# A second attention whose scores stand by keys on partitions, with GpSimd subtracting the maximum

## The reference

```python
x = x + _L0_conv_ref(_gn(x), ...)        # 8 heads, mask, depthwise convolution
t = _to_tokens(x)
t = t + _L1_attn_ref(_ln_t(t), Wq, bq, Wk, bk, Wv, bv)
t = t + _L1_ffn_ref(_ln_t(t), ...)       # two of eight experts for each image

def _L1_attn_ref(x, Wq, bq, Wk, bk, Wv, bv):
    q, k, v = x @ Wq + bq, x @ Wk + bk, x @ Wv + bv
    scores = jnp.einsum('btd,bsd->bts', q, k)
    attn = jax.nn.softmax(scores, axis=-1)
    return jnp.einsum('bts,bsd->btd', attn, v)
```

## Time and profile before

| | us |
|---|---|
| median of three executions | 3510.87 |
| the profiled execution | 3511.96 |
| its span, first to last instruction | 3510.2 |
| TensorE busy | 3403.2 (97%) |
| VectorE busy | 2635.0 (75%) |
| ScalarE busy | 2015.6 (57%) |
| GpSimd busy | 1645.1 (47%) |
| second attention, first scores to last values | 2575.4 to 3347.8 |

### The profile page before, as it was taken

One profiled execution on the slowest core, in us unless ns is written; L12 is line 12 of the kernel. 1 busy time (PEld: TensorE's weight loads), 2 busy tenths in 40 slices (PEclk: granted clock), 3 DMA queues, 4 the chain that ended last, 5 costly groups with the idle time before them and its releaser, 6 DMA issues. The chain is left out here.

```text
span 3510.2 us, 94134 instructions
## 1 busy us (share of the span) xinstructions
PE 3403.2 (97%) x30646; PEld 2643.6 (75%) x30646; DVE 2635.0 (75%) x6494; ACT 2015.6 (57%) x3642; POOL 1645.1 (47%) x863
## 2 busy tenths in 40 slices
PE   8799999999999999999999999999799999999978
PEld 5477777777777777777777777777578888888867
DVE  8688888888888888888888888888666675654457
ACT  4466666666666666666666666666435454455533
POOL 5566656556556556656656655655400001005112
PEclk9899999999999999999999999999899999999989
DMA  7642242234224224222422422222331020100011
GB/s 266 194 133 94 72 135 94 72 106 123 73 99 129 72 92 136 73 92 100 109 92 94 115 92 94 81 91 94 106 99 58 15 85 4 39 1 1 1 44 42
DMA packets 111794, 308.21 MB, mean 88 GB/s; under 512 B 11592, under 2 KB 72955, under 8 KB 91163
## 3 DMA queue, kind: packets, MB, share of 16 engines
q1 hardware_dynamic: 110629, 306.27, 27.9%
q10 hardware_dynamic: 1054, 0.48, 0.1%
HBM read 252.38 MB, written 54.31 MB: 87 GB/s over the span
## 5 line engine op out<-in xcount | busy, mean ns | idle before, releaser
L730 ACT ACTIVATE c_PT<-c_Tps 128x512 f32<-128x512 f32 x2592 | 1428.3, 604 | 877.8 <-PE c_Tps L860 815.7
L795 DVE CUSTOM_DVE_ANT_0 c_S<-c_Sps,mask_tiles 128x768 f32<-128x768 f32 x1728 | 1619.3, 956 | 412.6 <-PE c_Sps L849 371.8
L698 POOL TENSOR_SCALAR c_S<-c_S,c_row_max 128x2304 f32<-128x2304 f32 x576 | 1414.0, 2455 | 950.6 <-DVE c_row_max L806 950.6
L860 PE MATMUL c_Tps<-ident,c_S 128*128 128x128 f32 x10368 | 1400.8, 273 | 4.1 <-ACT c_PT L730 4.1
L860 PEld LDWEIGHTS c_Tps<-ident,c_S 128*128 128x128 f32 x10368 | 1229.7, 140 | 152.1 <-ACT c_PT L730 9.7
L849 PE MATMUL c_Sps<-c_K,c_Q 96*128 (+1 forms) x3456 | 854.6, 328 | 29.0 <-DVE c_part_max L795 14.6
L873 PE MATMUL c_Ops<-c_PT,c_V 128*32 128x256 f32 x10368 | 619.2, 382 | 0.8 <-ACT c_PT L730 0.8
L873 PEld LDWEIGHTS c_Ops<-c_PT,c_V 128*32 128x32 f32 x10368 | 307.4, 109 | 243.6 <-issue 51.1
L849 PEld LDWEIGHTS c_Sps<-c_K,c_Q 96*128 96x128 bf16 x3456 | 315.2, 98 | 188.4 <-issue 144.1
L1463 DVE TENSOR_SCALAR_CACHE_REDUCE l_S<-l_Sps,l_v 128x384 f32<-128x384 f32 x432 | 259.8, 618 | 252.9 <-PE l_Sps L1264 249.3
L1148 ACT ACTIVATE ln2T<-l_Tps 128x384 f32<-128x384 f32 x432 | 196.5, 491 | 363.6 <-PE l_Tps L1287 363.6
(11 more groups left out here) (223 smaller groups left out, 1644.2 us busy)
## 6 DMA issues: line engine op xcount, KB each, us to landing
mask_tiles<-in_mask SPq DMA_DIRECT2D x144, 1152.0 KB, 7.7
numerators<-c_O SPq DMA_DIRECT2D x288, 64.0 KB
mask_tiles<-numerators SPq DMA_DIRECT2D x7, 2304.0 KB, 8.5
q_parts<-c_PT SPq DMA_DIRECT2D x12, 576.0 KB, 4.4
k_parts<-c_PT SPq DMA_DIRECT2D x12, 576.0 KB
c_Q<-q_parts SPq DMA_DIRECT2D x71, 96.0 KB
c_vpad<-v_padded SPq DMA_DIRECT2D x8, 756.0 KB, 14.8
c_K<-k_parts SPq DMA_DIRECT2D x7, 864.0 KB, 8.6
```

The lines of the kernel that those rows point to most:

```text
L698: pool.tensor_scalar(S[:, slot, :], S[:, slot, :], -1.0, row_max[:, slot:slot + 1], ALU.mult, ALU.add).then_inc(shifted, 1)
L730: act.activation(dst, src, ACT.Exp, scale=-1.0).then_inc(exp_done, 1)
L795: dve.tensor_tensor_reduce(out=S[:, r % ROW_SLOTS, cols(CH, c)].rearrange("p (k n) -> p k n", k=2), in0=Sps[:, n % S_SLOTS, :, 0:GW], in1= ...
L860: last = pe.transpose(Tps[:, g % T_SLOTS, cols(P, k)], S[:, (2 * b + t) % ROW_SLOTS, cols(P, kt)], ident[:, :])
```

## The change

For a query tile, the scores now come out with keys on partitions: 18 matmuls of 128 keys (stationary, from lnT) by 128 queries (moving, read straight from qT; no staging copy), in the orientation in which the values need them. The 18 transposes of the exponentials go. ScalarE copies the raw scores from PSUM to one of three slots of SBUF (the two rows of S and the former PT). The maximum of a query now lies across keys on partitions and across 18 tiles, so:

- VectorE takes the maximum over nine key tiles, twice (half_maximum, a tensor_reduce whose inner step is 128 floats), and joins the two (key_maximum, 128 x 128).
- TensorE turns that (turn_max); VectorE reduces it to one number a query and spreads it over 128 columns (query_maximum); TensorE turns it back (spread_max); ScalarE copies it to SBUF (take_shift).
- GpSimd subtracts it from the 18 x 128 scores in two tensor_tensor of 1152 columns (subtract_max), and ScalarE makes the exponentials in two halves.

A column of ones behind the values gives the sum (129 columns instead of 128). The scores run two tiles ahead instead of one (AHEAD = 2), and PSUM has four banks for them (T_SLOTS = 4) and two for the turned maxima. GpSimd's bias groups are spread over the tiles 0 to 5, and normal over the tiles of the last image, at most two groups a tile. In the loop of VectorE the preparation still stands behind the tiles of the same numbers, now after key_maximum.

```diff
-            def scores(b, qt, t, groups=range(NG)):
...
-                    pe.matmul(Sps[:, g % S_SLOTS, 0:GW], q_tile[:, t, :], lnT[:, bass.ds((b % 2) * N + g * GW, GW)],
...
+                        last = pe.matmul(Tps[:, (n + g) % T_SLOTS, cols(P, k)], lnT[:, bass.ds((b % 2) * N + (g * GB + k) * P, P)], query_tile,
+                                         start=True, stop=True)
...
-                        block_t = pe.transpose(Tps[:, g % T_SLOTS, cols(P, k)], S[:, t, cols(P, g * GB + k)], ident[:, :])
...
+                if j + AHEAD < ALL:
+                    scores(j + AHEAD, range(4))
+                    spread_max(j + 1)
+                    scores(j + AHEAD, range(4, NG))
+                values(j, 0)
+                if j + AHEAD == ALL:
+                    spread_max(j + 1)
+                values(j, 1)
+                if j + AHEAD < ALL:
+                    turn_max(j + AHEAD)
...
+            def subtract_max(j):
+                pool.wait_ge(shift_in, j + 1)
+                for half in HALVES:
+                    part = keys_by[j % P_SLOTS][:, half.start:half.stop, :]
+                    pool.tensor_tensor(part, part, shift[:, :, :].to_broadcast([P, len(half), P]), ALU.subtract).then_inc(shifted, 1)
...
+                if j + AHEAD < ALL:
+                    take_scores(j + AHEAD, range(4))
+                if j + 1 < ALL:
+                    take_shift(j + 1)
+                if j + AHEAD < ALL:
+                    take_scores(j + AHEAD, range(4, NG))
+                if j + 1 < ALL:
+                    for half in range(2):
+                        exponentials(j + 1, half)
+                if b + 1 < B and qt == TRANSPOSE - 1:
+                    deviations(b + 1)
...
+            def half_maximum(j, half):
+                dve.wait_ge(t_taken, scores_at(j) + NG * (half + 1) // 2 + T_SLOTS)
+                part = keys_by[j % P_SLOTS][:, HALVES[half].start:HALVES[half].stop, :].rearrange("p t q -> p q t")
+                dve.tensor_reduce(half_max[:, half, :], part, AX.X, ALU.max).then_inc(half_step, 1)
...
+            def key_maximum(j):
+                dve.wait_ge(half_step, 2 * (j + 1))
+                dve.tensor_tensor(key_max[:, j % 2, :], half_max[:, 0, :], half_max[:, 1, :], ALU.max).then_inc(key_max_ready, 1)
...
+            for j in range(ALL):
+                b, qt = j // TILES, j % TILES
+                if j:
+                    take_row(j - 1)
...
+                if j and j + 1 < ALL:
+                    query_maximum(j + 1)
+                if j:
+                    row_statistics(j - 1)
+                if j + AHEAD < ALL:
+                    half_maximum(j + AHEAD, 0)
+                    half_maximum(j + AHEAD, 1)
+                    key_maximum(j + AHEAD)
+                if b + 1 < B:
+                    if qt == 0:
+                        invert(b + 1)
...
```

More of the change, by code:

```diff
@@ L1324, in _ @@
[L1324 to L1330 removed]
+            scores(0, range(NG))
+            scores(1, range(3))
```

436 lines of the change are left out of this document (208 added, 228 removed).

## The result

| | before | after |
|---|---|---|
| median (lowest to highest), us | 3510.06 (3508.09 to 3511.88) | 3518.18 (3516.83 to 3520.58) |
| ratio, with its 95% interval | | 1.0024 (1.0014 to 1.0035) |
| span of the profiled execution, us | 3510.2 | 3516.5 |
| scores to scores in a plain tile, us | 9.86 | 9.22 |
| first scores of the stage to the end of the last value, us | 772.4 | 783.1 |

The forecast was 3519. The stage is 10.7 us longer, and it began 4.0 us earlier, at 2571.45 instead of 2575.41; the rest of the program is as it was. So the 4.0 us lie within that scatter, and I count them as no part of the change.

What follows compares the result with a forecast made beforehand. TensorE was taken to bound the second attention. Plain tiles and ends -64, side work +61, GpSimd in the last image +12 gave +9 on 3511.96 us; 3519 was forecast, range 3455 to 3565, the forecast's own 3500 to 3538.

Steps and rivals of the forecast that it cites:

- 69 plain tiles: Second attention, tiles without side work: each falls from 9.86 to 8.95 us, 63 us less in all.
- the ends: Filling and draining of the tile pipe: 30 us against 31.5 before, counted as 1 us less.
- side work of three images: VectorE's preparation of the next image delays spread_max and TensorE: 19.7 us an image, 2 in the filling pipe, 61 us.
- GpSimd in the last image: normal, 4.7 us for two groups, makes ten tiles 10.4 us long against 8.95: 12 us more.
- TensorE's part: A tile falls from 90 to 74 passes, 8.3 us at 0.112 each; 112 us would go if all else were hidden.
- The rival that no passes are saved: TensorE's 128-column matmuls with fresh weights are slower than wide ones, so the passes do not go; chance 0.04.
- GpSimd's half: One subtract_max tensor_tensor of 1152 columns: 2.5 us, ends 2.3 and 3.0, so 5.0 us a tile.
- The strided rival: half_maximum's 128-float step is slow: at twice 1.34 us plain tiles stay, stalled ones grow some 16 us, 3535; chance 0.06.
- Key_maximum first: Rival: key_maximum gets its turn at the boundary of GpSimd's halves; tile 8.45 us, time 3485, range 3465 to 3500; chance 0.24.
- the forecast's state: key_maximum asks just after GpSimd began its second half and stands until it ends; tile 8.95 us; chance 0.33.
- the stall before the transposes of ln: normalise waits behind the square root, itself behind tile 11's exponentials: TensorE stands 5.8 us in each of three images.
- the slower rival: TensorE's clock halves at stalls, 5 us each, 15 or twice that: 3535 to 3550; chance 0.17 together with dear GpSimd halves.

Runs made afterwards that it cites:

- the last kernel: No key_maximum, side work ahead of half_maximum, bias six tiles earlier, last-image normal() moved from GpSimd to VectorE, against the kernel before: 3438.47 us, ratio 0.9797.

## Why the prediction held, and where it was lucky

The sum was -64 + 61 + 12 = +9, and the stage gave +10.7. Its terms, from the spacings of tiles:

| term | predicted, us | measured, us |
|---|---|---|
| 69 plain tiles | 69 x (8.95 - 9.86) = -63 | 69 x (9.22 - 9.86) = -44 |
| the ends | -1 | 33.9 - 31.4 = +2.5 |
| side work of three images | 59 + 2 = +61 | 98.3 - 52.8 = +45.5 |
| GpSimd in the last image | +12 | 14.8 - 8.0 = +7 |
| sum | +9 | +11 |

The measured terms of the last two rows are what the tiles are longer than plain ones, after less before. They hold TensorE's passes for the preparation and the expert transposes, which both kernels have. The ends after are 21.35 us to the start of tile 1 (2571.45 to 2592.80), where 19 were predicted, and 12.5 for the last two tiles, where 11 were.

The total is right by luck in the sizes: 19 us too much gain from the tiles stood against 16 us too much loss from the side work and 5 in the last image, and the ends are 3.5 us worse. The mechanisms were the ones named.

**TensorE's part.** A pass is 0.112 us for 128-column matmuls with fresh weights too: the 24 score passes of the plain tile start at 3332.81 and the next matmul at 3335.49, 2.68 / 24 = 0.112. 75 passes fill a tile of 8.37 and 74 one of 8.26, in the kernels where TensorE is the bound. The rival that no passes are saved falls.

**GpSimd's half, the mis-sized term.** 2.5 us were taken between 2.3 and 3.0, by proportion from 768 columns; 2.64 were measured. A tile is two halves and 3.95 by the prediction's own layout. In the plain tile above GpSimd starts 3.62 us behind the first scores (3332.81), works 5.25, and the next scores start 0.36 after it, at 3342.04: 5.25 + 3.98 = 9.23. So the 3.95 was right, and 0.27 x 69 = 19 us is the error of the tiles, nearly all of it in the halves. The row of 768 columns reads one bf16 input beside an f32; whether that makes it cheaper, no run tells.

The estimate of 2.6 from the Trainium skill (GPSIMD Engine Reference, Performance versus the Vector engine) was nearer, and its sum, 14 us longer, would have had this term nearly right. In plain proportion the page's 4497 ns for 2048 columns make 2.53 at 1152, an estimate that is no better than the row's.

**Who waits for whom.** Shown by the kernel without key_maximum: 55 us of waits go with one instruction. The Trainium skill (SBUF — State Buffer, Who interferes with whom) exempts tensor_reduce from the lock, which no row of before showed; the trace after agrees, with 2.12 to 2.23 us for all 144 half_maximum, most of them beside a running GpSimd half. The bias locks as predicted: the first product of finish_half starts 0.1 us behind a bias and takes 2.16 us instead of 1.34 (at 2823.94). What the prediction leaves out are operations with one input and output both in SBUF, which stand too: the copy and the tensor_scalar of the last kernel.

**half_maximum, wrong and without effect.** 1.34 us were taken from sum_half, 2.20 measured. The strided rival had it at two times with plain tiles unchanged, and that holds: with reading in order alone the time is 2.2 us less, and the intervals of the two ratios overlap, because it is not enough to reach the boundary. The 16 us put on stalled tiles for it do not show.

**Key_maximum first.** The margin was not the 0.1 us of the prediction but 0.85, since half_maximum is slow. So this kernel was further from the rival than the prediction thought; but, as the kernel that reads in order shows, without the stride it is still in the forecast's state, at the very boundary. In plain tiles the mechanism is as described: asked 0.4 us ahead of the boundary VectorE gets the turn, asked at the boundary it stands 2.75 us. The tile that follows is 8.26, where 8.45 was worked out: the loop through ScalarE and GpSimd does not bind. The 3485 of the rival is 3476 in the kernel that is in that state (which leaves part of the reduction out).

**Side work, the order right, the size too large.** The waits behind it, without TensorE's passes, are 16.3 us an image where 19.7 were predicted, and 3.1 in the filling pipe where 2 were, 52 in all. From these comes off what the prediction put at nothing: the kernel before had 1.5 us of waits an image in the same tiles, and its passes for the preparation took some 0.7 us more, together 6.5 us in three images. Per image, now: invert 0.63 us (1.4 predicted), the sums 2.6 and 2.75 (3.4 each), the finishes 1.5 and 0.7 (2.3, 1.3), statistics 1.5 (2.1), the stall before the transposes of ln 6.55 (5.8). The short ones are each 0.6 to 0.8 less. Half of this can be read off. spread_max stands 2.84 us behind turn_max in the plain tile (2.7 predicted) and take_row with query_maximum takes 1.17 (3332.52 to 3333.69; 1.25), so side work may reach 1.65 us into the tile, not 1.45: 0.2. And the tile behind such a one is often 9.01 instead of 9.22, another 0.2. The rest stays open. The kernels with pieces (26 us less) and with the work ahead of half_maximum (28 less) show that this term is real.

**The stall before the transposes of ln.** The order on ScalarE was as described; moved ahead it gives back 8 us of 3 x 6.55 = 20. The other part is normalise itself.

**The last image.** +12 predicted. The waits in its spacings are 8 us (7 against the kernel before, which had one of its own there); the kernel without normals is 10 us faster. Tiles of 10.4 at the start were predicted. There is one of 9.92 and one of 12.65, of which 1.5 us are the half clock, and then five with 0.7 excess, with plain ones between them: GpSimd catches up after one or two tiles each time.

**The clock, a wrong statement that cost the sum little.** "1.00 in all of it" is false: 0.50 for 6.8 us at each of the three stalls, as the slower rival had it, and for 3.4 us in three other places. But the rival's price, 5 us at each stall, is not there. The transposes at half clock take 4.75 us for 18, and normalise feeds them in 4.71; TensorE would have stood anyway. What is paid are the nine score passes behind them, 1.51 us instead of 1.01. Here the half clock lies under a wait that is there for another reason. Where full work follows the wait it does not: 1.5 us at 3210 in this kernel, 2.5 in the last kernel at 2786.

## What to carry to other kernels

Where VectorE and GpSimd share a stage, look for the small VectorE operation that stands behind GpSimd: one with two inputs in SBUF, or, as the last kernel shows, a copy or tensor_scalar from SBUF to SBUF while GpSimd reads two tensors. Its price is the rest of whatever GpSimd is running, however short it is itself, a whole instruction where it just misses the boundary between two, and it pays to give its work to a reduction over data that another engine has put in PSUM. When an edit brings a cross-engine chain close to the period of the bottleneck, everything that was hidden in the slack of the other engines moves onto the path, so the edit has to come with a new order for that work: here the change alone lost 8 us, and with the lock, the place of the side work and the normals put right it gained 71. A forecast by terms should be checked by terms, since a right total can hold two wrong ones.

## What the hardware showed that was not expected

A tensor_reduce on VectorE that steps 512 bytes between elements takes 2199 ns for 1152 elements a partition, and 1352 in order of memory: 1.91 against 1.17 ns an element.

At the boundary of two GpSimd instructions that follow each other at once, VectorE got the turn in plain tiles when it asked 0.4 us ahead (key_maximum 0.56 us, the median of 72), and did not when it asked at the boundary (2.75 us). One tile is 0.95 us longer for it, and the kernel 40 us. Where GpSimd had come to the first of the two without a pause, asking 1.1 to 2.3 us ahead did not get the turn in seven tiles (3.8 to 5.0 us).

VectorE operations with one input in SBUF can stand behind GpSimd as well. Beside GpSimd's tensor_tensor of 1152 columns a copy of two columns took 2.48 us instead of 0.17 and a tensor_scalar of 128 columns 2.80 instead of 0.34, both in the last kernel; tensor_reduce over 1152 columns took at most 2.25 in all kernels. Beside GpSimd's normal, which reads one tensor, the copy took 0.17 to 0.30 us in the changed kernel.

The clock fell at idle times of TensorE under 4 us: 6.8 us at 0.50 behind 3.61 us of idle time with groups of three transposes after it, and 3.4 us at 0.50 behind 2.59 us of idle time in a full stream of matmuls (3209.77). With the square root moved, single idle times of 1.15 and 0.81 us and the same slow groups, it fell all the same. What decides it, no run here tells.
